# The V projection's copies out of PSUM move from the vector engine to the scalar engine

## The reference

```
x      = (sequence - mean) / sqrt(var + EPS) * ln_gamma + ln_beta
q,k,v  = split_heads(x @ Wq.T + bq), split_heads(x @ Wk.T + bk), split_heads(x @ Wv.T + bv)
scores = einsum(q, k) / sqrt(64)
scores = sigmoid(scores - mu) * exp(scores);  scores = scores / sum(scores)
out    = einsum(scores, v) @ Wo.T + bo
x      = layernorm(sequence + out)
x      = layernorm(x + ffn(x))
```

## Time and profile before

| | us |
|---|---|
| median of 2 runs | 6621.5 |
| lowest and highest run | 6609.13, 6633.86 |
| the profiled execution | 6607.29 |
| its slowest core, core 6, first to last instruction | 6605.4 |
| its other cores | 6588.0 to 6602.0 |

### The profile page before, as it was taken

The page is one execution under the profiler, slowest core; times in us unless marked ns, Lnnn a source line. Parts: engine busy times, 40 slices in busy tenths (PEclk is TensorE's granted clock), DMA queues, the critical chain, the costliest instruction groups (busy, mean ns, idle before and its releaser), DMA issues.

```text
span 6605.4 us, 68606 instructions; the slowest of 8 cores (6588.0 to 6605.4 us)
## 1 busy us (share of the span) xinstructions
PE 4670.5 (71%) x15170; PEld 1234.7 (19%) x15252; DVE 3408.8 (52%) x3706; ACT 4762.6 (72%) x5797; POOL 837.6 (13%) x1540
## 2 busy tenths in 40 slices
PE   3687887767777777777777677777767777775544
PEld 0232335521111111111111111111111111111212
DVE  2112122356666665666666566666656666665342
ACT  0333435779999986999999599999959999993111
POOL 2234443210000000000000000000000000000111
PEclk7899996555555556555555655555565555556777
DMA  6223223421111111111111111111111111111211
GB/s 215 91 57 94 83 84 105 120 59 30 31 31 32 32 36 38 31 31 31 31 32 41 33 32 32 30 32 32 35 39 32 32 32 30 32 32 31 67 61 64
DMA packets 182632, 332.78 MB, mean 50 GB/s; under 512 B 37354, under 2 KB 119274, under 8 KB 182260
## 3 DMA queue, kind: packets, MB, share of 16 engines
q0 software_dynamic: 73664, 185.17, 9.1%
q1 hardware_dynamic: 108596, 143.22, 7.9%
HBM read 277.39 MB, written 50.86 MB: 50 GB/s over the span
## 4 chain that ended last, share of the span: by engine, by line
ACT 48%; PE 18%; DVE 13%; issue 12%; DMA 5%; POOL 3%; ACTq 0%; DVEq 0%; SPq 0%; POOLq 0%
ACT tbf L862 35%; ACT ebf L865 11%; DVE wbf L979 5%; PE pr_ps L1290 3%; POOL vd L512 3%; PE o_ps L963 2%; PE st_ps L931 2%; PE ktp L531 2%; DMA ktd<-ktev 2%; DMA vd<-vev 2%; DVE dinvb L996 1%; PE o_ps L967 1%; PE pp L1089 1%; PE pjp L479 1%; PE ktp L564 1%
## 5 line engine op out<-in xcount | busy, mean ns | idle before, releaser
L979 DVE SCALAR_TENSOR_TENSOR wbf<-tbf,ebf 128x1024 bf16<-128x1024 bf16 (+1 forms) x2560 | 2591.7, 1013 | 1811.2 <-ACT ebf L865 1741.7
L862 ACT ACTIVATE tbf<-st_ps,mubc 128x1024 bf16<-128x1024 f32 (+1 forms) x2560 | 2949.0, 1152 | 346.0 <-PE st_ps L935 213.7
L865 ACT ACTIVATE ebf<-st_ps,ln2b 128x1024 bf16<-128x1024 f32 (+1 forms) x2560 | 2957.1, 1155 | 0.0
L963 PE MATMUL o_ps<-wbf,vbx 128*65 128x512 bf16 (+1 forms) x2560 | 1326.4, 518 | 1142.8 <-DVE wbf L979 1107.9
L967 PE MATMUL o_ps<-wbf,vbx 128*65 128x512 bf16 (+1 forms) x2560 | 1376.5, 538 | 0.0
L931 PE MATMUL st_ps<-qt_sb,ktb 64*128 64x512 bf16 (+1 forms) x2560 | 1298.7, 510 | 82.2 <-ACT ebf L865 74.0
L935 PE MATMUL st_ps<-qt_sb,ktb 64*128 64x512 bf16 (+1 forms) x2560 | 1314.2, 516 | 0.0
L895 POOL DMA_DIRECT2D ktb<-ktd x640 | 343.1, 536 | 4355.5 <-PE st_ps L935 4278.8
L963 PEld LDWEIGHTS o_ps<-wbf,vbx 128*65 128x65 bf16 x2560 | 334.2, 131 | 2214.1 <-issue 2185.3
L931 PEld LDWEIGHTS st_ps<-qt_sb,ktb 64*128 64x128 bf16 x2560 | 253.6, 100 | 1702.5 <-issue 1677.5
L501 DVE CAST vev<-pjp 128x512 bf16<-128x512 f32 x128 | 88.5, 691 | 641.1 <-PE pjp L483 483.9
(11 more groups left out here) (192 smaller groups left out, 2430.6 us busy)
## 6 DMA issues: line engine op xcount, KB each, us to landing
vbx<-vd SPq DMA_DIRECT2D x640, 132.0 KB, 2.1
ktb<-ktd POOLq DMA_DIRECT2D x640, 128.0 KB, 2.3
xg<-xkv SPq DMA_DIRECT2D x64, 512.0 KB, 7.2
vd<-vev POOLq DMA_DIRECT2D x512, 33.0 KB, 4.3
ktd<-ktev POOLq DMA_DIRECT2D x128, 128.0 KB, 2.1
woh_sb<-wos POOLq DMA_DIRECT2D x80, 128.0 KB, 2.7
xq<-xkv SPq DMA_DIRECT2D x16, 512.0 KB, 5.8
wch<-wrs POOLq DMA_DIRECT2D x32, 256.0 KB, 3.1
```

The lines of the kernel that those rows point to most:

```text
L862: ac.inc(s.activation(tbuf[k % WBUF][:].rearrange("p (h w) -> p h w", h=2)[:, :, 0:W], srcv, AF.Tanh, bias=mubc[:], scale=0.5))
L865: a2.inc(s.activation(ebuf[k % WBUF][:].rearrange("p (h w) -> p h w", h=2)[:, :, 0:W], srcv, AF.Exp, bias=ln2b[:], scale=1.0))
L963: tn.matmul(o_ps[par][0][0:65, 0:W], vb[c2 % 4][:, 132 * j:132 * j + 65], wbuf[k2 % WBUF][:, 0:W], start=(k2 == 0), stop=(k2 == KS - 1))
L979: s1.inc(v.scalar_tensor_tensor(vw(wbuf[k % WBUF][:]), vw(tbuf[k % WBUF][:]), 1.0, vw(ebuf[k % WBUF][:]), op0=AX.add, op1=AX.mult))
```

## The change

The eight V copies of a group leave DVE (`emit_vevac` is gone) and are made by ACT, in `emit_vevacs_act`, as Identity activations with the same source and destination. ACT's program now begins each group g from 1 on with the V copies of group g-1, ahead of the statistics of group g; those of group 15 stand after the loop, ahead of the last K copies. POOL's stores of V wait for ACT instead of DVE. PE's V product number idx (two for each tile) waits for the copies of the whole tile (idx-3)//2, on ACT's semaphore, where it waited for the copy of product idx-3 on DVE's. The tables count the new signals: `vVEa` for ACT, `gVv` for the V stores, and `cvx` no longer counts DVE's.

```diff
@@ emit_vproj
                         for hf in range(2):
-                            bk = (2 * t + hf) % 3
-                            if bk in last_pj_evac:
-                                tn.wait_ge(dv.sem, last_pj_evac[bk])
+                            idx = 2 * t + hf
+                            bk = idx % 3
+                            if idx >= 3:
+                                tn.wait_ge(ac.sem, vVEa[(idx - 3) // 2])
@@
-                def emit_vevac(t):
-                    @blk.vector
-                    def _(v, t=t):
-                        for hf in range(2):
-                            bk = (2 * t + hf) % 3
-                            v.wait_ge(pe.sem, pV[t] - (1 - hf))
-                            if t >= 2:
-                                v.wait_ge(dVs[t % 2].sem, gV[t - 2])
...
-                            ins = v.tensor_copy(dst, src)
-                            dv.inc(ins)
-                            last_pj_evac[bk] = dv.v
-                            v.wait_ge(dv.sem, dv.v)
-                        vVE[t] = dv.v
@@ emit_vstore
-                        g.wait_ge(dv.sem, vVE[t])
+                        g.wait_ge(ac.sem, vVEa[t])
@@ tables
-                        cvx += 2
...
+                    if g >= 1:
+                        for t in range(4 * (g - 1), 4 * (g - 1) + 4):
+                            cax += 2
+                            vVEa[t] = cax
@@ ACT's program
+                    def emit_vevacs_act(s, gp):
+                        for t in range(4 * gp, 4 * gp + 4):
+                            for hf in range(2):
+                                bkp = (2 * t + hf) % 3
+                                s.wait_ge(pe.sem, pVv[t] - (1 - hf))
+                                if t >= 2:
+                                    s.wait_ge(dVs[t % 2].sem, gVv[t - 2])
+                                dst = v_ev[t % 2][:, 4 * hf:4 * (hf + 1), :].rearrange(
+                                    "p a (h x) -> p a h x", h=2)[:, :, :, 0:64]
+                                srcp = pj_ps[bkp][:].rearrange(
+                                    "p (a h x) -> p a h x", a=4, h=2)
+                                ch(s, ac, s.activation(dst, srcp, AF.Identity))
                     for g in range(NG4):
+                        if g >= 1:
+                            emit_vevacs_act(s, g - 1)
                         for t in range(4 * g, 4 * g + 4):
                             s.wait_ge(dXs[t % 4].sem, dXv[t])
...
+                    emit_vevacs_act(s, NG4 - 1)
                     emit_ktq_evacs(s, NG4 - 1)
```

More of the change, by code:

```diff
@@ L516, in _ @@
                         gV[t] = dVs[t % 2].v
+                        assert dVs[t % 2].v == gVv[t]
                 def emit_ktproj(hh):
@@ L619, in build @@
                 cax = acB
+                vVEa = {}
                 for g in range(NG4):
+                    if g >= 1:
+                        for t in range(4 * (g - 1), 4 * (g - 1) + 4):
+                            cax += 2
+                            vVEa[t] = cax
                     for t in range(4 * g, 4 * g + 4):
@@ L638, in build @@
                         vEa[t] = cax
+                for t in range(4 * (NG4 - 1), 4 * (NG4 - 1) + 4):
+                    cax += 2
+                    vVEa[t] = cax
                 hp2 = NG4 - 1
@@ L648, in build @@
                        for (kk, hh_, d2_) in ktq_seq]
+                gVv = {}
+                dvsB = [dVs[0].v, dVs[1].v]
+                for t in range(NT):
+                    gVv[t] = dvsB[t % 2] + 128 * (t // 2 + 1)
                 @blk.scalar
                 def _(s):
+                    def emit_vevacs_act(s, gp):
[10 more added lines that the diff above has]
+                                ch(s, ac, s.activation(dst, srcp, AF.Identity))
+                            assert ac.v == vVEa[t]
                     for g in range(NG4):
+                        if g >= 1:
+                            emit_vevacs_act(s, g - 1)
                         for t in range(4 * g, 4 * g + 4):
@@ L733, in build @@
                         emit_vproj(tt2)
-                        emit_vevac(tt2)
                         emit_vstore(tt2)
```

## The result

The changed kernel takes 6675.2 us (median of 33 runs), the kernel before 6625.1 (median of 32). The ratio is 1.0077, with an interval of 1.0065 to 1.0089: 50 us slower, no change at the level of 2%, and on the side that was forecast. The profiled execution of the changed kernel took 6678.4 us. Its cores span 6642.1 to 6676.9. Core 0 spans 6642.1, 54.1 more than before.

What follows compares the result with a forecast made beforehand. A chain of V stores, V copies, small operations, K stores, K copies and PE bounds a group. Fourteen groups at +4.25 (+59.5) and group 14's +11.1 make +70.6 on 6607.3: 6677.9 us, range 6620 to 6737.

Steps and rivals of the forecast that it cites:

- V part: Stretch from a group's first `xnt_g` copy to the fourth tile's first V copy; taken as 23.3 us.
- K part: Stretch from the fourth tile's first V copy to the next group's first `xnt_g` copy; 26.17 us before, 29.2 forecast.
- What bounds the stage: Projection stage: a chain of V stores, V copies, small operations, K stores, K copies and PE sets a group's end.
- The copy: One V copy on ACT takes 0.60 us against DVE's 0.69; worth 0.2 us for a group at most.
- The V part stays: Claim that the move leaves this stretch alone: 24.2 us in group 7, 22.4 in group 14, mean 23.3.
- first rival: V stores land sooner, all cores get core 0's 19.4 us V part; some +13 us, 6620; chance 0.15.
- G: Moment in a group when the fourth tile's first V copy starts; forecast 22 to 24 us after the first `xnt_g` copy.
- Steps 1 to 7 of the K part: From G: V copies, statistics, small operations, Ln to K copy, PE restart, five K products, next `xnt_g` copy; 29.2 us.
- Where a stall goes: Statistics fill ACT's wait for K stores, so 10.4 us lateness adds only 3.0; K stores land in 3 us.
- threshold of 5.6 us: K store landing time up to which the third K copy's wait costs nothing.
- late round: Rival: K stores land in 7.9 us, not 3; +2.3 to +4.2 a group, 6710 to 6737; chance 0.16.
- The rule on DMA queues: Engines go round queues packet by packet, so loads hold a K store only a few packets: 3 us rather than 8.

Runs made afterwards that it cites:

- second measurement: Both kernels again, unedited, on chip 12: the changed kernel took 6676.2 us, the kernel before 6592.4, ratio 1.0121.
- loads last: `xg` loads held until a group's last K copy: in the changed kernel 6645.4 us (1.0081), in the kernel before 6513.2 us (0.9903).
- order restored: Changed kernel with the next group's statistics placed between ACT's V copies: 6598.5 us, ratio 1.0015.
- wait-only kernel: Kernel before, one wait added: ACT starts a group's statistics only after DVE's last V copy of the group before; 6677.1 us, ratio 1.0127.

## Why the prediction was right, point by point

The forecast was 6677.9, a loss of 70.6 us on core 6's own sum, and the measured median is 6675.2. The loss itself came out at 50 us, and at 84 in the second measurement. The sum's mechanism was right. Two of its terms were off and partly cancelled each other: over groups 4 to 13 core 6's V part is 19.7 us where I took 23.3, and its K part 31.5 where I had 29.2. What was left of the error, core 6's own loss in groups 0 to 14 being 52.4 us and not 70.6, was made up by my starting point, a profiled execution of 6607.3 that lies 18 us under the median of the kernel before. So that the forecast comes within 3 us of the measured time is luck; what it got right is the direction, the rough size of the loss (70.6 us against 50 to 84) and its cause.

- *What bounds the stage.* Right. The chain of V stores, last V copy, small operations, K copies and K stores set the pace: the runs that shorten one link of it (four K buffers, loads last) gained 71 us at once, measured in the kernel before.
- *The copy.* 0.60 us was taken, 0.60 is in the rows. The Trainium skill, "ScalarE: Activation LUTs", section "Rules for kernel authors", puts VectorE up to about 3 times ahead in bf16. That doesn't show in these copies, whose source is fp32 in PSUM: 0.60 us on ACT and 0.69 on DVE. With the order restored, ACT's copies cost next to nothing (1.0015).
- *The V part stays.* Wrong: 23.3 us taken for core 6, 19.7 measured over groups 4 to 13 (24.0 before) and 19.8 in group 7. "The V part moves by over 2 us" was one of my own signs that the prediction is wrong, and on this core it came true. My first rival, with a chance of 0.15, had just this: all cores get core 0's V part. Cores 0, 3, 4 and 7 had a V part of 19.9 us before and have 19.8 after; cores 1, 2, 5 and 6 went from 23.8 to 20.2. I had built the sum on one of these. The rival's time, 6620, did not come, because the K part grew everywhere. V stores of a group's second tile land sooner, so the wait for V stores fell from 138 to 79 us. The step that failed is "G is set by POOL's issues and the landing of tile 2's stores, neither of which the change touches". The wait-only kernel has the same 20.0 us, so it comes with the schedule and not with ACT's copies. The rival's reason, the shifted loads, has the rows against it as far as a core's own loads go: group 14 of the changed kernel has 20.1 us (996.38 to 1016.44) and the kernel before 22.4 there, in both cases with no loads to come. More on this in the last section.
- *Steps 1 to 7 of the K part.* 29.2 forecast, 31.4 measured as mean of all cores. In group 7: statistics 2.7 us after G instead of 1.6, because the second V copy waited 1.32 us for its product, a term that I had left out: since G came earlier, it stood nearer to PE's own pace. Statistics 10.4 us, small operations 1.4 up to Ln, Ln to K copy 0.8, K copy to PE 0.7: as forecast. PE's stall was 7.86 us, not some 12, because G came earlier while PE kept its pace. The first products ran at the 1.2 GHz level as forecast: six matmuls took 2.77 us (675.45 to 678.22), where eight take 1.89 a little later.
- *Where a stall goes.* The term that was mis-sized. I took 3 us for the landing of a K store beside the loads; it was 4.6 us for the first and 5.9 for the second on the mean (5.9 and 6.7 in group 7 of core 6). And the threshold of 5.6 us that I worked out looked only at the third copy: the fourth, fifth and seventh copies wait too, each for the store two before it, and the last of these delays the next `xnt_g` copy. So some 2.2 us a group were lost although the first store stayed below the threshold on the mean. The run with the loads last brings 31.3 down to 29.1; the one with four buffers has 29.3. The price of a late round (2.3 us at least) was about right; its chance was 0.16.
- *The rule on DMA queues.* The first two K stores land in 4.6 and 5.9 us beside the loads, and in 2.2 with the loads elsewhere. So the loads cost a store 2.4 to 3.7 us, more than I drew from the Trainium skill ("DMA: Bandwidth & Descriptors", section "Queues, rings and completion order", a DMA engine goes round its queues packet by packet). No run shows single packets.
- *Group 14.* +11.1 forecast, +9.2 measured (996.38 to 1046.03 is 49.65, before 40.47).
- *The sum.* 14 groups at +4.25: forecast a group of 52.5 us. Measured (996.38 - 208.77 - 68.8)/14 = 51.3, so +43.2 us in the 14 groups where I had +59.5.
- *The leading cores.* Wrong: I had core 0 losing 1 us a group. Its V part stayed at 20 us and its K part grew from 27.9 to 31.8, and its span grew by 54.1 us, more than core 6's 48.5.
- *What would show it.* The statistics after G, the first K copy 14.6 us after it on the mean, DVE waiting for ACT: seen. "One stall in place of two" holds nearly (7.86 us and not 12, and 1.04 is left of the second). "G 22 to 24 us after the first `xnt_g` copy" was wrong (19.8), and "the wait for K stores under 60 us" was wrong: 148. That sign would have told from the profile alone which term was off.

## What to carry to other kernels

An engine with 500 idle us is a good home for new work only if the work doesn't wait in front of something that the idle time was hiding. Before moving an operation, list what stands behind it in the new engine's program and what was waiting for that; here one wait in the wrong place cost 85 us with no copy moved, and the moved copies, once the order was right, some 6. And when a sum has a threshold below which a delay is free, work it out for every instruction of the loop that waits on the same resource, not for the first.

## What the runs showed that I had not expected

- A K store takes 2.2 us to land with the queues free, 2.8 behind V stores, 4.6 beside loads, and 7.5 with both. In the last case it lands near the end of the loads: in the kernel before on chip 12, issued 28.5 us after the group's first `xnt_g` copy, it lands at 36.0, the last load at 37.5; in the kernel with three buffers, issued at 27.2, at 36.6 and 38.7. Holding the loads until the last K copy gives 1.0% in the kernel before.
- A cure in one stretch can come back in the next. Three V buffers took 2.5 us a group off the V part and the K part grew by 0.9, in a kernel that also had a third K buffer, which should have shortened it. The two profiles are of different chips (14 and 12).
- Neighbouring cores differ. In the kernel before, one core of each pair (0 and 1, 2 and 3, 4 and 5, 6 and 7) has early V stores and late K stores and the other the reverse. The table gives the last V store of a group's second tile and the first K store of a group, from issue to landing, as means over groups 4 to 13. On chip 12 the cores fall into the same two kinds (2.8 and 8.7 us for cores 0, 2, 5 and 7; 5.3 and 6.3 for the others). This speaks for the neighbour's transfers as what a landing depends on, beside the core's own. No run tests it.

| core | 0 | 1 | 2 | 3 | 4 | 5 | 6 | 7 |
|---|---|---|---|---|---|---|---|---|
| before: V store | 3.1 | 7.0 | 7.1 | 3.3 | 2.6 | 6.5 | 7.3 | 3.3 |
| before: K store | 10.3 | 6.3 | 6.5 | 9.5 | 10.0 | 6.0 | 6.7 | 10.1 |
| changed: V store | 2.3 | 3.9 | 1.8 | 2.2 | 2.0 | 3.0 | 2.0 | 2.0 |
| changed: K store | 4.3 | 4.6 | 4.9 | 4.5 | 4.6 | 4.3 | 4.8 | 4.8 |

- The same V store takes 2.1 to 2.5 us as mean of all cores in all six profiles in which the statistics stand behind the V copies, and 3.6 to 5.0 in all eight in which they stand beside or between them, whoever makes the copies and wherever the loads are. With the loads last in the kernel before, these are through 7 us after the first `xnt_g` copy, the store is issued at 18, and it still takes 3.9. So how fast this store lands goes with the place of the statistics, and a core's own loads are not the reason; what is, stays open.
- The kernel before has a stage of 1036 us in one measurement and 1015 in the other, the changed one 1088 in both. Why also stays open.
